# The first two groups' matrices fetched one by one with register addresses, beside the gathers, in a kernel on one core

## The chip, the core and the metric

The kernel runs on one core of a Trainium2 chip. The metric is the device time of one execution in microseconds (us). The core has five engines with an instruction queue each: TensorE (PE in the rows; its weight loads are PEld), VectorE (DVE), ScalarE (ACT), GpSimd (POOL) and SyncE (SP), which only waits and issues transfers. They meet at semaphores. Transfers (DMAs) are issued by SP, ACT or POOL and carried by 16 DMA engines that all of them share.

## The reference, cut to what is computed

```python
# x (32, 32, 256) f32; itok (32,) int32 in 1..198; L0_cond_weights (200, 32, 32)
w = weights[conditions]                       # one 32x32 matrix per batch, chosen by itok
y = einsum('bct,bcd->bdt', x, w)              # the mixing, 32 batches
h = silu(y @ w_gate) * (y @ w_up)             # w_gate, w_up (256, 1024)
h_sparse = of every 4 neighbours of h along the last axis, the 2 largest in magnitude, the others 0
out = x + h_sparse @ w_down                   # w_down (1024, 256)
```

## The kernel before

The 32 batches are eight groups `g` of four (`NG = 8`, `NB = 4`), since four batches of 32 channels fill 128 partitions. Groups 0 to 3 are half 0 and groups 4 to 7 half 1; each half is 512 columns wide (`TH`). The 256 entries of `T` are two blocks `k` of 128. Every product of the two big layers is made of float32r parts: a value is split into a high part, written by ScalarE as a copy (`high_weights`, `high_y`), and a low part, the difference, written by VectorE (`low_weights`, `low_y`), and three of the four products of the parts are summed.

The start of the program, on which everything here rests, runs as follows.

- SP issues `cond` (the chosen rows' numbers), `x[0]` (half 0 of x, 512 KB) and the k = 0 piece of `w_gate` (256 KB, lines 173 to 176). It then waits until the first gather has landed (`mix_in[0]`) and issues the k = 1 piece and the first 512 KB of `w_up`, waits for the latter, and issues `x[1]`, the second halves of the weights and `w_down`.
- VectorE adds the two halves of `cond` to row numbers (line 439). GpSimd then issues two indirect DMAs (line 206), one per half: each gathers for all 16 batches of its half the matrices, in chunks, from `table`. VectorE puts the gathered chunks in place with a 32x32-block transpose (line 351, signalled by `transposed`) and spreads them over a block diagonal (`mix_diag`, line 359, in three spans of groups).
- TensorE starts with 12 matmuls on a zeroed tile `warm` (line 520), whose results nobody reads. It then waits for the first `w_gate` piece's high part and mixes half 0: for k = 0 batch by batch, 16 matmuls of 32 rows and 32 columns (`mixing_by_batch`, line 529), for k = 1 with the block diagonal, one matmul per group (`mixing`, line 543). `mixed` counts when a k is ready; ScalarE and VectorE split it into `y_hl`.
- `first_gates` (line 570) makes the gate products of pairs 0 and 1 together (12 matmuls of 512 columns), and `gate_up(n)` (line 558) the others: 16 pairs `n`, each one block of 128 hidden columns in one half. Half 1 is mixed ahead of pair 3 (`MIX_PAIR`). For each pair ScalarE makes the silu, VectorE the product, and both then find the two largest of four. The down products (line 600) close the program.

In a row of the trace a float32 matmul of the mixing appears as two records, so 16 matmuls stand there as 32.

All orders are written out by hand; each engine works its instructions off in that order. The weight pieces and who waits for them come from this table and function:

```python
PIECES = [(0, w, k, k + 1) for w in range(2) for k in range(KT)] + \
         [(q, w, 0, KT) for q in range(1, NQ) for w in range(2)]
def pieces_until(q, w, k):
    return 1 + max(i for i, piece in enumerate(PIECES) if piece[:2] == (q, w) and piece[2] <= k)
```

Of the kernel before, what the change touches and what calls it, by code (L numbers as in the profile page):

```python
# [5 lines left out]
NQ = 2  # L6
M = 4
CHUNKS = 8

def adaln_ffn(nc: bass.Bass, x: bass.AP, x_t: bass.AP, cond: bass.AP, table: bass.AP,
              w_gate: bass.AP, w_up: bass.AP, w_down: bass.AP, out: bass.AP):

# [9 lines left out]
    P = 128  # L23
    i32 = mybir.dt.int32
    _, _, GH, T = x.shape
    NH = 2
# [10 lines left out]
    WARM_START = 12  # L37
    LAST = len(UNITS) - 1
    MIX_PAIR = 3
    SENT = 2  # L40
# [7 lines left out]
    with ctx:  # L48
# [27 lines left out]
        mix_w = h[:, 1, 1, 0:NG * D].rearrange("p (g o d) -> p g o d", o=1, d=D)  # L76
# [12 lines left out]

        cond_in = sem("cond_in")  # L90
        x_in = [sem(f"x_in{i}") for i in range(NH)]
        w_in = [[None, sem("gate_in1")], [sem(f"up_in{q}") for q in range(NQ)]]
# [6 lines left out]
        transposed = sem("transposed")  # L99
        diag_done = sem("diag_done")  # L100
# [38 lines left out]
        def split_y(part, half, k, end):  # L139
# [5 lines left out]
        SPANS = [slice(0, 2), slice(2, 4), slice(4, 8)]  # L145

        PIECES = [(0, w, k, k + 1) for w in range(2) for k in range(KT)] + \
                 [(q, w, 0, KT) for q in range(1, NQ) for w in range(2)]

        def pieces_until(q, w, k):  # L150
            return 1 + max(i for i, piece in enumerate(PIECES) if piece[:2] == (q, w) and piece[2] <= k)

        GATE_PIECES_END = PIECES.index((1, 0, 0, KT)) + 1

# [4 lines left out]
        UNFINISHED = 3  # L159
# [7 lines left out]
        def raw_piece(q, w, k, end):  # L167

            return raw_w[w][:, q, k:end].rearrange("p k (j g) -> p k j g", j=M)

        @block.sync
        def _(sp):
# [11 lines left out]
            sp.dma_start(raw_w[0][:, 1], w_gate[1].rearrange("k p n -> p k n")).then_inc(w_in[0][1], 16)  # L184
            sp.dma_start(raw_w[1][:, 1], w_up[1]).then_inc(w_in[1][1], 16)
# [4 lines left out]
            for i, (half, k, begin, end, _) in enumerate(OUTPUTS[:-1]):  # L190
                if i != UNFINISHED:
# [37 lines left out]
        def _(act):  # L229
# [43 lines left out]
            for k in range(KT):  # L273
                high_weights(*PIECES[k])
                high_y(*Y_PIECES[k])
# [398 lines left out]
```

## Time and profile before

| | us |
|---|---|
| three timed runs | 80.46, 80.88, 80.88 (median 80.88) |
| the profiled execution's own time | 80.44 |
| its span, first to last instruction | 78.6 |
| TensorE busy | 74.5 (95% of the span) |
| VectorE, ScalarE, GpSimd busy | 62.1, 41.7, 8.6 |

The profiled execution's time is 1.84 us longer than its span; that part lies outside of what the instructions show. Busy time of an engine says how full it is, and the chain of work that ended last says on which engine the end depends. A row of the timeline gives start, duration, engine, line, operation, the tile written and the tiles read, the count that was merged into the row, and in brackets how long the engine had been idle and what released it. SPq and ACTq are the sequencers' own rows: there a DMA row is the issuing, not the transfer.

### The profile page before, as it was taken

What the parts mean: (1) busy time and instruction counts of PE and PEld (TensorE: products, weight loads), DVE (VectorE), ACT (ScalarE), POOL (GpSimd) and SP (SyncE); (2) the same over time, 40 slices, a digit from 0 to 9 for tenths busy, and PEclk for the clock granted to TensorE, in tenths of its full rate; (3) what the DMA queues carried; (4) which work ended last, traced back from release to release, by engine and by line L of the source; (5) the groups of instructions that cost most, each with busy time, mean ns of one, the idle gap of its engine ahead of it and who ended that gap; (6) DMA issues with size and microseconds to landing.
All of it is one profiled execution on the core that took longest, in us unless ns stands there. A gap on an engine that the chain in (4) does not pass through costs nothing.

```text
span 78.6 us, 1020 instructions
## 1 busy us (share of the span) xinstructions
PE 74.5 (95%) x362; PEld 59.5 (76%) x362; DVE 62.1 (79%) x91; ACT 41.7 (53%) x61; POOL 8.6 (11%) x18
## 2 busy tenths in 40 slices
PE   3999999999999999999999999999999999999950
PEld 1338778888888888888888888888888888888840
DVE  0017691699879999599999979999999999994460
ACT  6122753869453375599897769789380402730000
POOL 5550000000000013000713000006200000000000
PEclk9999999999999999999999999999999999999999
DMA  0857559984900004900099990003995000003333
GB/s 1 250 183 201 232 154 381 413 377 92 425 33 0 0 0 79 188 0 0 15 194 200 194 198 13 4 0 60 200 177 96 0 0 0 8 0 138 137 142 118
DMA packets 3221, 9.64 MB, mean 123 GB/s; under 512 B 496, under 2 KB 752, under 8 KB 2960
## 3 DMA queue, kind: packets, MB, share of 16 engines
q0 software_dynamic: 928, 3.28, 21.9%
q1 hardware_dynamic: 2144, 6.16, 21.8%
q10 hardware_dynamic: 144, 0.13, 0.5%
q8 instruction: 3, 0.05, 0.2%
q14 instruction: 2, 0.02, 0.1%
HBM read 5.38 MB, written 1.05 MB: 82 GB/s over the span
## 4 chain that ended last, share of the span: by engine, by line
PE 95%; POOL 1%; DVE 1%; issue 0%; POOLq 0%
PE banks L558 52%; PE banks L600 28%; PE banks L520 6%; PE banks L543 4%; PE banks L570 4%; PE banks L529 1%; POOL warm L199 1%; DVE gate_raw L435 1%; POOLq L663 0%
## 5 line engine op out<-in xcount | busy, mean ns | idle before, releaser
L558 PE MATMUL banks<-y_hl,up_hl 128*128 128x512 f32 x96 | 24.2, 389 | 0.0
L600 PE MATMUL banks<-h_hl,down_hl 128*128 128x512 f32 (+1 forms) x102 | 22.0, 376 | 0.0
L558 PE MATMUL banks<-y_hl,gate_hl 128*128 128x512 f32 x84 | 21.4, 390 | 0.0
L600 PEld LDWEIGHTS banks<-h_hl,down_hl 128*128 128x128 f32 x102 | 18.5, 188 | 3.6
L558 PEld LDWEIGHTS banks<-y_hl,up_hl 128*128 128x128 f32 x96 | 18.0, 188 | 3.8
L558 PEld LDWEIGHTS banks<-y_hl,gate_hl 128*128 128x128 f32 x84 | 15.7, 188 | 3.2
L243 ACT ACTIVATE silu<-banks 128x512 f32<-128x512 f32 x16 | 9.6, 597 | 12.4 <-PE banks L558 12.1
L384 DVE TENSOR_TENSOR h<-banks,silu 128x512 f32<-128x512 f32 x12 | 8.3, 689 | 4.4 <-ACT silu L243 4.4
L264 ACT ACTIVATE h_hl<-h 128x1024 fp32r<-128x1024 f32 (+1 forms) x8 | 6.7, 843 | 3.9 <-DVE h L420 3.9
L420 DVE SCALAR_TENSOR_TENSOR h<-count,h 128x512 f32<-128x512 bf16 x12 | 7.9, 687 | 0.1
L520 PE MATMUL banks<-warm 128*128 128x512 bf16 x12 | 4.8, 586 | 1.3 <-POOL warm L199 1.3
L250 ACT ACTIVATE x_sb<-h 128x512 f32<-128x512 f32 x8 | 4.9, 626 | 1.7 <-DVE h L384 1.7
L435 DVE TENSOR_TENSOR gate_raw<-banks,gate_raw 128x512 f32<-128x512 f32 (+1 forms) x6 | 3.5, 602 | 2.4 <-PE banks L600 2.3
L214 POOL DMA_DIRECT2D down_hl<-down_raw x2 | 1.8, 919 | 31.5 <-ACT down_hl L259 31.5
L219 POOL DMA_DIRECT2D h_hl<-h x4 | 3.7, 928 | 13.4 <-ACT h_hl L268 13.4
L395 DVE TENSOR_TENSOR far<-x_sb 128x1024 bf16<-128x1024 f32 x4 | 4.9, 1222 | 0.2
L395 DVE TENSOR_TENSOR far<-a_even 128x1024 bf16<-128x1024 f32 x4 | 4.9, 1220 | 0.2
L520 PEld LDWEIGHTS banks<-warm 128*128 128x128 bf16 x12 | 1.6, 141 | 4.1 <-issue 2.7
L268 ACT ACTIVATE h_hl<-h 128x1024 fp32r<-128x1024 f32 x4 | 4.2, 1054 | 0.0
L233 ACT ACTIVATE gate_hl<-gate_raw 128x512 fp32r<-128x512 f32 (+1 forms) x3 | 2.3, 771 | 3.6 <-DMA gate_raw<-in_w_gate 3.6
L264 ACT ACTIVATE h_hl<-up_raw 128x1024 fp32r<-128x1024 f32 x2 | 2.1, 1054 | 3.2 <-DVE up_raw L420 3.2
L351 DVE STREAM_TRANSPOSE h<-h 128x128 f32<-128x128 f32 x2 | 0.8, 406 | 3.1 <-DMA h<-in_table,rows_sb 3.1
(39 smaller groups left out, 68.1 us busy)
## 6 DMA issues: line engine op xcount, KB each, us to landing
h_hl<-h POOLq DMA_DIRECT2D x4, 512.0 KB, 6.1
x_sb<-in_x SPq DMA_DIRECT2D x2, 512.0 KB, 3.4
up_raw<-in_w_up SPq DMA_DIRECT2D x2, 512.0 KB, 4.7
down_raw<-in_w_down SPq DMA_DIRECT2D x1, 1024.0 KB, 7.8
gate_raw<-in_x_t SPq DMA_DIRECT2D x1, 1024.0 KB, 4.8
down_hl<-down_raw POOLq DMA_DIRECT2D x2, 512.0 KB, 5.0
out<-gate_raw SPq DMA_DIRECT2D x3, 256.0 KB, 2.4
gate_raw<-in_w_gate SPq DMA_DIRECT2D x2, 256.0 KB, 3.3
```

Source lines behind the costliest of these rows:

```text
L219: pool.dma_start(h_hl[:, u, LO, j:end], hs[u][:, j:end], accum_op=ALU.add).then_inc(h_lo_sent[u][j // 2], 16)
L243: nc.scalar.activation(silu[:, n % 3], gate_bank(n), ACT.Silu).then_inc(silu_done, 1)
L250: nc.scalar.activation(a[u % 2][:, j], hs[u][:, j], ACT.Abs).then_inc(abs_done, 1)
L264: nc.scalar.activation(h_hl[:, u, HI, j:end], hs[u][:, j:end], ACT.Copy).then_inc(h_hi, 1)
L268: nc.scalar.activation(h_hl[:, u, LO, j:end], hs[u][:, j:end], ACT.Copy, scale=-1.0).then_inc(h_neg, 1)
L384: nc.vector.tensor_tensor(hs[u][:, j], up_bank(n), silu[:, n % 3], ALU.mult).then_inc(h_done, 1)
L395: step(nc.vector.tensor_tensor(far[:, j - 2::2], au[:, 0:2], au[:, j:j + 1].broadcast_to([P, 2, TH]), ALU.is_ge))
L420: nc.vector.scalar_tensor_tensor(hs[u][:, j], count[:, j], bound, hs[u][:, j], op, ALU.mult).then_inc(masked, 1)
L435: nc.vector.tensor_tensor(xt_sb[:, k, cols], bank[:, begin:end], xt_sb[:, k, cols], ALU.add).then_inc(out_done, 1)
L520: nc.tensor.matmul(gate_bank(0), warm[:, 0:P], warm[:], start=True, stop=True)
L558: last = nc.tensor.matmul(dst, w_hl[w][:, s, q, k, j], y_hl[:, m, half, k], start=i == 0, stop=i == len(terms) - 1)
L600: last = nc.tensor.matmul(bank[:, begin:end], down_hl[:, s, q, j, k * P:(k + 1) * P], h_hl[:, u, m, j, begin:end], start=(q, j, m, s) == f ...
```

## The change

Groups 0 and 1 of half 0 (eight batches; `EARLY = 2`) get their matrices in another way. The host also sends the list of chosen numbers (`cond_list`) and the unchunked table (`matrices`). ScalarE reads the four numbers of group 0 from `cond_list` in HBM into registers, and issues one 4 KB transfer per batch whose source address is a register. SP does the same for group 1, after its first three transfers. `early_in[g]` counts the four transfers of a group. The host rolls the list of the gathers by two groups, so that the first gather brings groups 2 to 5 and the second groups 6, 7, 0 and 1 (the last two into room that nobody reads).

Around that, five things move:

- VectorE zeroes `warm` in place of GpSimd, and TensorE's warm matmuls are 8 in place of 12.
- ScalarE's table load and first silu stand behind its four transfers.
- TensorE's mixing of half 0 goes group by group: group 0 for both k, then group 1, and then groups 2 and 3, for k = 0; only these two wait for the gathered matrices (`transposed`). The k = 1 matmuls of groups 1 to 3 follow. VectorE makes the diagonal of group 0 alone first, and those of groups 1 to 3 in one instruction behind the transpose.
- The first half of the weights comes in smaller pieces: for k = 0 and k = 1 of `w_gate` only the first 256 of 512 columns (128 KB each in place of 256 KB), then the first 256 columns of `w_up`, then the rest of both. There are seven pieces in place of six, and ScalarE and VectorE split them in that order. The second half comes in four transfers in place of two.
- The last output transfer but one is issued by ScalarE and the last by SP; before, ScalarE issued the last.

```diff
-    WARM_START = 12
+    WARM_START = 8
+    EARLY = 2
...
+        PIECES = [(0, 0, k, k + 1, 0, 2) for k in range(KT)] + [(0, 1, 0, KT, 0, 2)] + \
+                 [(0, w, 0, KT, 2, M) for w in range(2)] + [(1, w, 0, KT, 0, M) for w in range(2)]
+        LATER = KT + 3
...
-        SPANS = [slice(0, 2), slice(2, 4), slice(4, 8)]
+        SPANS = [slice(0, 1), slice(1, GH), slice(GH, NG)]
...
             sp.dma_start(x_sb[:, 0:GH, :], x[0]).then_inc(x_in[0], 16)
-            sp.dma_start(raw_w[0][:, 0, 0], w_gate[0, 0]).then_inc(first_in[0], 16)
+            sp.dma_start(raw_w[0][:, 0, 0, 0:2 * P], w_gate[0, 0, 0]).then_inc(first_in[0], 16)
+            _, chosen = nc.values_load_multi_w_load_instructions(
+                cond_list[:, NB:2 * NB], engines=(mybir.EngineType.SP,),
+                skip_runtime_bounds_check_because="the transfers check their own bounds")
+            for b in range(NB):
+                sp.dma_start(mix_w[b * C:(b + 1) * C, 1, 0],
+                             matrices[bass.ds(chosen[b], 1)].rearrange("o c d -> (o c) d")).then_inc(early_in[1], 16)
             sp.wait_ge(mix_in[0], 16)
             for k in range(1, KT):
-                sp.dma_start(raw_w[0][:, 0, k], w_gate[0, k]).then_inc(first_in[k], 16)
-            sp.dma_start(raw_w[1][:, 0], w_up[0]).then_inc(w_in[1][0], 16)
-            sp.wait_ge(w_in[1][0], 16)
+                sp.dma_start(raw_w[0][:, 0, k, 0:2 * P], w_gate[0, 0, k]).then_inc(first_in[k], 16)
+            sp.dma_start(raw_w[1][:, 0, :, 0:2 * P], w_up[0, 0].rearrange("k p n -> p k n")).then_inc(up_in, 16)
+            for w, weights in enumerate((w_gate, w_up)):
+                sp.dma_start(raw_w[w][:, 0, :, 2 * P:4 * P],
+                             weights[0, 1].rearrange("k p n -> p k n")).then_inc(rest_in[w], 16)
+            sp.wait_ge(up_in, 16)
             sp.dma_start(x_sb[:, GH:NG, :], x[1]).then_inc(x_in[1], 16)
...
-            nc.gpsimd.memset(warm[:], 0.0).then_inc(warm_zero, 1)
...
+            _, chosen = nc.values_load_multi_w_load_instructions(
+                cond_list[:, 0:NB], engines=(mybir.EngineType.Activation,),
+                skip_runtime_bounds_check_because="the transfers check their own bounds")
+            for b in range(NB):
+                act.dma_start(mix_w[b * C:(b + 1) * C, 0, 0],
+                              matrices[bass.ds(chosen[b], 1)].rearrange("o c d -> (o c) d")).then_inc(early_in[0], 16)
             act.wait_ge(warm_zero, 1)
             nc.scalar.activation(silu[:, 0, 0:2], warm[:, 0:2], ACT.Silu).then_inc(table_loaded, 1)
...
+            nc.vector.memset(warm[:], 0.0).then_inc(warm_zero, 1)
             dve.wait_ge(cond_in, 16)
+            dve.wait_ge(blocks_marked, 1 + NB)
             nc.vector.tensor_tensor(rows_sb[:], cond_sb[:, 0:NH], cond_sb[:, NH:2 * NH], ALU.add).then_inc(rows_done, 1)
-            dve.wait_ge(blocks_marked, 1 + NB)
+            diagonal(SPANS[0])
             transpose_rows(0)
-            diagonal(SPANS[0])
             diagonal(SPANS[1])
...
+            def first_mixing():
+                mixing_by_batch(0)
+                mixing(0, 1)
+                mixing_by_batch(1)
+                for g in range(EARLY, GH):
+                    last = mixing_by_batch(g)
                 last.then_inc(mixed, 1)
+                for g in range(1, GH):
+                    last = mixing(g, 1)
+                last.then_inc(mixed, 1)
```

How the first instructions of ScalarE stand before, in its queue from the start on. `silu<-warm` is the instruction that makes the table be loaded, `gate_hl<-gate_raw` the high part of the first weight piece:

```order
L272 ACT_TABLE_LOAD
L272 ACTIVATE silu<-warm 128x2 [waits warm_zero]
L233 ACTIVATE gate_hl<-gate_raw 128x512 [waits first_in0]
L237 ACTIVATE y_hl<-banks 128x512 [waits mixed]
L233 ACTIVATE gate_hl<-gate_raw 128x512 [waits first_in1]
```

And how they stand now; `h<-in_matrices` is one batch's matrix, and an ISA row the arithmetic on its address:

```order
L302 TENSOR_LOAD in_cond_list_ptr
L302 TENSOR_LOAD in_cond_list
L306 ISA
L306 DMA h<-in_matrices 32x32
L306 ISA
L306 DMA h<-in_matrices 32x32
L306 ISA
L306 DMA h<-in_matrices 32x32
L306 ISA
L306 DMA h<-in_matrices 32x32
L309 ACT_TABLE_LOAD
L309 ACTIVATE silu<-warm 128x2 [waits warm_zero]
```

Ten rows now stand ahead of the table load; the high part of the first weight piece, now 128x256, follows behind the silu as before.

How TensorE's queue stands before, from its start to the mixing of k = 1:

```order
L520 MATMUL banks<-warm 128x512 [waits warm_zero]
L520 MATMUL banks<-warm 128x512 x11
L529 MATMUL banks<-h,x_sb 128x32 [waits transposed,x_in0,w_hi]
L529 MATMUL banks<-h,x_sb 128x32 x15
L543 MATMUL banks<-h,x_sb 128x128 [waits diag_done,x_in0]
```

And the same place now:

```order
L560 MATMUL banks<-warm 128x512 x7
L572 MATMUL banks<-h,x_sb 128x32 [waits x_in0,early_in0,w_hi]
L572 MATMUL banks<-h,x_sb 128x32 x3
L582 MATMUL banks<-h,x_sb 128x128 [waits diag_done]
L572 MATMUL banks<-h,x_sb 128x32 [waits early_in1]
L572 MATMUL banks<-h,x_sb 128x32 x3
L572 MATMUL banks<-h,x_sb 128x32 [waits transposed]
L572 MATMUL banks<-h,x_sb 128x32 x3
L572 MATMUL banks<-h,x_sb 128x32 [waits transposed]
L572 MATMUL banks<-h,x_sb 128x32 x3
L582 MATMUL banks<-h,x_sb 128x128 [waits diag_done]
```

The wait for `transposed`, which stood ahead of all 16 small matmuls, now stands ahead of the last eight, and there are waits for the two groups' transfers ahead of the others.

## Rows read from the trace of the kernel before

**Rows 1.** The page: busy time by engine, and the last chain's shares.

```profile
PE 74.5 (95%) x362; PEld 59.5 (76%) x362; DVE 62.1 (79%) x91; ACT 41.7 (53%) x61; POOL 8.6 (11%) x18
...
PE 95%; POOL 1%; DVE 1%; issue 0%; POOLq 0%
```

**Rows 2.** The last chain in order of time (start, duration, what), its first pieces.

```profile
1.33 4.83 PE banks L520 x12
6.16 0.08 issue
6.24 1.09 PE banks L529 x32
7.33 1.09 PE banks L543 x8
8.42 2.91 PE banks L570 x12
11.33 5.46 PE banks L558 x24
```

**Rows 3.** The timeline up to 5.5 us, from several engines.

```profile
0.75 0.52 POOL L199 MEMSET warm<- 128x512 bf16 x1 [0.29 <-POOLq L663]
0.75 0.38 SPq L173 DMA_DIRECT2D cond_sb<-in_cond  x1
0.75 1.28 ACT L272 ACT_TABLE_LOAD   x1 [0.75 <-PEq L663]
1.19 0.42 SPq L175 DMA_DIRECT2D x_sb<-in_x  x1
...
1.66 0.42 SPq L176 DMA_DIRECT2D gate_raw<-in_w_gate  x1
...
2.05 0.20 ACT L272 ACTIVATE silu<-warm 128x2 f32<-128x2 bf16 x1
...
2.86 1.19 POOL L206 DMA_INDIRECT h<-in_table,rows_sb  x1 [0.97 <-DVE rows_sb L439]
...
5.14 0.15 PEld L520 LDWEIGHTS banks<-warm 128*128 128x128 bf16 x1 [0.28 <-issue]
5.37 0.63 ACT L233 ACTIVATE gate_hl<-gate_raw 128x512 fp32r<-128x512 f32 x1 [3.12 <-DMA gate_raw<-in_w_gate]
5.57 0.10 PEld L520 LDWEIGHTS banks<-warm 128*128 128x128 bf16 x1 [0.27 <-issue]
```

**Rows 4.** The timeline from 5.6 to 8.5 us, from several engines.

```profile
5.60 0.33 SPq L180 DMA_DIRECT2D gate_raw<-in_w_gate  x1
5.68 0.41 DVE L351 STREAM_TRANSPOSE h<-h 128x128 f32<-128x128 f32 x1 [3.11 <-DMA h<-in_table,rows_sb]
...
6.21 1.01 PEld L529 LDWEIGHTS banks<-h,x_sb 32*128 32x128 f32 x32 [0.54 <-ACT gate_hl L233]
...
7.39 0.60 ACT L237 ACTIVATE y_hl<-banks 128x512 fp32r<-128x512 f32 x1 [1.39 <-PE banks L529]
8.09 0.69 DVE L373 TENSOR_TENSOR y_hl<-banks,y_hl 128x512 fp32r<-128x512 f32 x1 [0.60 <-ACT y_hl L237]
...
8.44 0.63 ACT L233 ACTIVATE gate_hl<-gate_raw 128x512 fp32r<-128x512 f32 x1 [0.45 <-DMA gate_raw<-in_w_gate]
```

**Rows 5.** DMA issues: KB each and median us from issue to landing.

```profile
x_sb<-in_x SPq DMA_DIRECT2D x2, 512.0 KB, 3.4
...
out<-gate_raw SPq DMA_DIRECT2D x1, 128.0 KB, 1.9
...
cond_sb<-in_cond SPq DMA_DIRECT2D x1, 2.0 KB, 1.6
```

**Rows 6.** Stretches, us: each engine's busy time (records), granted clock, DMA share, GB/s.

```profile
3.00:4.00 1.00, 1.00 (x4) 0.44 (x3) 0.00 (x0) 0.00 (x0) 1.00 (x1) 1.00 1.02 375
4.00:4.50 0.50, 0.50 (x3) 0.17 (x2) 0.00 (x0) 0.00 (x0) 0.20 (x2) 1.00 1.00 389
...
5.00:5.50 0.50, 0.50 (x2) 0.15 (x1) 0.00 (x0) 0.13 (x1) 0.35 (x1) 1.00 0.03 8
```

**Rows 7.** Shapes in the first 20 us: busy us, mean ns of one.

```profile
L366 DVE TENSOR_TENSOR gate_hl<-gate_raw,gate_hl 128x512 fp32r<-128x512 f32 x2 | 1.4, 688 | 0.4 <-ACT gate_hl L233 0.4
...
L233 ACT ACTIVATE gate_hl<-gate_raw 128x1024 fp32r<-128x1024 f32 x1 | 1.1, 1052 | 0.0
...
L359 DVE TENSOR_TENSOR h<-h,own_block 128x256 f32<-128x256 f32 x2 | 0.8, 422 | 0.0
```

**Rows 8.** The timeline where the up weights are split, and VectorE's first product.

```profile
9.67 1.15 ACT L233 ACTIVATE up_hl<-up_raw 128x512 fp32r<-128x512 f32 x2
...
13.44 0.69 DVE L384 TENSOR_TENSOR h<-banks,silu 128x512 f32<-128x512 f32 x1 [1.75 <-ACT silu L243]
```

**Rows 9.** The end of VectorE's work, and the outputs.

```profile
68.65 1.90 DVE L426 TENSOR_TENSOR h_hl<-h,h_hl 128x512 fp32r<-128x512 f32 x3
...
75.91 0.42 DVE L435 TENSOR_TENSOR gate_raw<-banks,gate_raw 128x256 f32<-128x256 f32 x1 [0.21 <-PE banks L600]
76.37 0.37 ACTq L335 DMA_DIRECT2D out<-gate_raw  x1
```

More of the change, by code:

```diff
@@ L99, in adaln_ffn @@
         transposed = sem("transposed")
+        early_in = [sem(f"early_in{g}") for g in range(EARLY)]
         diag_done = sem("diag_done")
@@ L142, in adaln_ffn @@
         Y_PIECES = [(0, k, k + 1) for k in range(KT)] + [(1, 0, KT)]
-        SPANS = [slice(0, 2), slice(2, 4), slice(4, 8)]
[L147 to L153, printed above, removed]
+        SPANS = [slice(0, 1), slice(1, GH), slice(GH, NG)]
+        GATE_PIECES_END = PIECES.index((1, 0, 0, KT, 0, M)) + 1
         OUTPUTS = [(0, 0, 0, TH, y_banks[:, 0]), (0, 1, 0, TH, y_banks[:, 1]),
@@ L189, in _ @@
             sp.dma_start(xt_sb, x_t).then_inc(xt_in, 16)
-            for i, (half, k, begin, end, _) in enumerate(OUTPUTS[:-1]):
-                if i != UNFINISHED:
+            for i, (half, k, begin, end, _) in enumerate(OUTPUTS):
+                if i not in (UNFINISHED, LEFT):
                     cols = slice(half * TH + begin, half * TH + end)
@@ L273, in _ @@
             for k in range(KT):
-                high_weights(*PIECES[k])
+                high_weights(k)
                 high_y(*Y_PIECES[k])
-            for piece in PIECES[KT:2 * KT]:
-                high_weights(*piece)
+            for i in range(KT, LATER):
+                high_weights(i)
             act.wait_ge(table_loaded, 1)
@@ L446, in _ @@
                 low_y(k)
-            for i in range(KT, 2 * KT):
+            for i in range(KT, LATER):
                 low_weights(i)
@@ L533, in mixing, with mixing_by_batch @@
-            def mixing(half, first=0):
-                pe.wait_ge(x_in[half], 16)
-                if half > 0:
-                    pe.wait_ge(y_lo, KT * half)
-                for k in range(first, KT):
-                    for i in range(GH):
-                        g = half * GH + i
-                        span = [groups.start <= g < groups.stop for groups in SPANS].index(True)
-                        if k == first and g == SPANS[span].start:
-                            pe.wait_ge(diag_done, span + 1)
-                        last = nc.tensor.matmul(y_banks[:, k, i * P:(i + 1) * P],
-                                                x_sb[:, g, k * P:(k + 1) * P],
-                                                mix_diag[:, g].rearrange("p b d -> p (b d)"),
-                                                start=True, stop=True)
+            def mixing_by_batch(g):
+                if g < EARLY:
+                    pe.wait_ge(early_in[g], 16 * NB)
+                else:
+                    pe.wait_ge(transposed, 1)
+                if g == 0:
+                    pe.wait_ge(x_in[0], 16)
+                for b in range(NB):
+                    rows = slice(b * C, (b + 1) * C)
+                    last = nc.tensor.matmul(banks[:, b, g * D:(g + 1) * D], x_sb[rows, g, 0:P],
+                                            mix_w[rows, g, 0], start=True, stop=True)
+                return last
@@ L547, in mixing, with second_mixing @@
+            def second_mixing():
+                pe.wait_ge(x_in[1], 16)
+                pe.wait_ge(y_lo, KT)
+                for k in range(KT):
+                    for g in range(GH, NG):
+                        last = mixing(g, k)
                     last.then_inc(mixed, 1)
@@ L613, in _ @@
                 if n == MIX_PAIR:
-                    mixing(1)
+                    second_mixing()
                 gate_up(n)
@@ L656 @@
         "cond": cond,
-        "table": table,
-        "w_gate": columns(inputs["L0_ffn_w_gate"]).transpose(0, 2, 1, 3),
+        "cond_list": _np.asarray(inputs["itok_B_1_198"]).reshape(1, B),
+        "table": chunks,
+        "matrices": table,
+        "w_gate": columns(inputs["L0_ffn_w_gate"]),
         "w_up": columns(inputs["L0_ffn_w_up"]),
```

105 lines of the change are left out of this document (62 added, 43 removed).

## The prediction, as it was put on record

> **What bounds the kernel now.** I read first the page's busy times and the shares of the last chain [rows 1]: TensorE is busy 95% of the span, and 95% of the chain lies on it. Then the chain in order of time [rows 2]: it enters TensorE at 1.33 us and from there goes from one group of matmuls to the next without a wait; to the end it leaves TensorE only for the last addition. So time is gained or lost only where TensorE's real work starts, or where it would come to wait. The change touches the start, so the timeline up to 8.5 us comes next [rows 3, 4]. Four things are to be seen there. The 12 warm matmuls are loaded 0.43 us apart (5.14 and 5.57) and end at 6.16. The gather starts on GpSimd at 2.86 and VectorE's transpose of what it brought runs 5.68 to 6.09. ScalarE's high part of the first weight piece runs 5.37 to 6.00, when that piece has landed. TensorE's first real weight load stands at 6.21. Three causes thus meet within 0.16 us, the warm matmuls (6.16), the gathered matrices (6.09) and the weight piece (6.00), and an edit that moves one alone brings nothing. Behind that, mixing takes 1.09 + 1.09 us and the first gates start at 8.42 [rows 2]. Those need the split y: ScalarE has it at 7.99 [rows 4], so TensorE's own 2.18 us of mixing is what ends last.
>
> **The edits with one answer.** The weight piece of 128 KB in place of 256 KB: the DMA engines were full and moved 375 to 389 GB/s [rows 6], so 0.128 MB less ahead of it is 0.34 us, and it lands at 5.37 - 0.34 = 5.03. Its high part has 256 columns: 1.05 us for 1024 against 0.63 for 512 [rows 7, 3] makes 0.42 for 256. The memset of the warm tile goes from GpSimd (0.52 us, [rows 3]) to VectorE, for which I take 0.25; TensorE starts at about 1.05 instead of 1.33. Eight warm matmuls at 0.43 end at 4.5. GpSimd's gather waits for the row numbers, not for its memsets, and stays at 2.86. The smaller later pieces cost VectorE and ScalarE one more instruction for the same number of elements, some 0.1 to 0.2 us. It is hidden by VectorE's wait of 1.75 us ahead of its first product, and the gate halves that were whole before now come behind the first half of up, which is why ScalarE's work on up, 9.67 before, can start earlier [rows 8]. Without that cover it would cost its 0.2. SP's two more issues at up to 0.47 stand ahead of w_down, which is needed long after. The swap of the last two outputs changes who issues, ScalarE in 0.37 before [rows 9]; SP's issues take 0.33 to 0.42 [rows 3, 4]: nothing.
>
> Then four transfers. SP's issues stand 0.44 and 0.47 us apart [rows 3]; with the address arithmetic I take 0.45. Behind them wait, on the same engine, the table load (1.28) and the silu (0.20) [rows 3], which before ran in the shadow of the transfers, and then the first high part, for which TensorE waits. The sum: 0.75 + 1.2 + 4 x 0.45 + 1.28 + 0.20 + 0.42 = 5.65. With the 0.12 us from the transpose's end to the first load (6.09 to 6.21, [rows 4]) TensorE begins at 5.77. The cover is nearly gone: the piece has landed at 5.03 and ScalarE comes free at 5.23. Group 0's transfers, the last of them issued at 3.30, land within 1.6 us if nothing is in the way, at 4.9, and by 6.1 if they are slowed to the gather's 2.6 or a little more; its diagonal of 128 columns takes under 0.42 [rows 7]. I take it as hidden.
>
> **SP's path, and the sum.** SP's third issue ends at 2.08 [rows 3]. Loads until 3.28, the fourth matrix issued at 3.28 + 3 x 0.45 = 4.63, landed 1.6 later [rows 5] at 6.23; the DMA engines are nearly idle by then (share 0.03 at 5.0 to 5.5, [rows 6]). TensorE goes on with group 1 at 6.35. By ScalarE's path it would be there at 5.77 + 0.27 (a quarter of the 1.09 of k = 0) + 0.27 (a quarter of the 1.09 of k = 1) = 6.31, so SP's path is last by 0.04. Groups 1 to 3 take three quarters of 1.09, to 7.17; the gathered matrices (6.09) are no longer waited for. The three k = 1 matmuls take 0.82 more, to 7.99. The split y is there at 7.17 + 0.06 + 0.60 [rows 4], about 7.9 with its signal, in time. The first gates start at 7.99 instead of 8.42: 0.43 us earlier. Behind SP's loads waits the k = 1 piece of w_gate; SP is free at 5.1, ahead of the 5.60 at which it was issued before, and half the size it lands earlier than the 8.44 of before [rows 4, 5]. From there on TensorE is full, and VectorE, whose first product comes 1.75 us of waiting after its last split [rows 8], moves with it, as does its end, which at 70.55 (68.65 + 1.90) lies over 5 us ahead of the last addition [rows 9].
>
> Against the profiled execution's own time: 80.44 - 0.43 = 80.0. That execution is the fastest of those shown; two of three runs are at 80.88, and 0.42 us is one warm matmul. If those runs had one slot more of slow matmuls ahead of the mixing, the change takes that away too, for its warm matmuls end 1.3 us before they are needed; I don't add it.
>
> **The ends.** If the loads are as short as the lower bound, the gather decides again: transpose ended at 6.09, half of the small matmuls (0.55) and three big ones (0.82) make 7.58, a gain of 0.84, and up to 0.34 more if the gather lands earlier by the smaller weight piece. The sum breaks even where both loads together take 1.63 us, and loses 1.57 at 3.2.
>
> **The rivals.**
> (a) *Nothing moves.* The loads take 1.25 to 2.0 us, so the matrices that were to come early come with the gathered ones or just behind, and the small pieces of work moved ahead only fill the wait. 80.1 to 80.8. For it: its whole cause is an operation that no row shows, and my sum is only 0.4 away. Against: even at 1.2 there are 0.43 in hand.
> (b) *The loads are long.* Beyond 2.0 us, ScalarE and SP hold up the first mixing, each behind its own loads; at 2.6 the first gates start at 9.39, and the time is 81.4. The page cited above would make it this. For it: two trips to memory in series; against: 2.6 is more than 1.6 of the whole small transfer without its issue, twice.
> (c) *TensorE's clock.* The granted clock stands at 1.00 in all stretches [rows 6], but warm matmuls of 512 columns come every 0.43 us, which is 1.2 GHz, and gates (12 in 2.91, [rows 2]) every 0.24, close to 2.4. So TensorE began at the low level and had risen by its first real work, after 4.9 us without a pause. Now it stops at 4.5 and idles for 1.3 us. If it is not at the high level then, half the speed costs the mixing (1.64 us of TensorE's work from 6.35) another 1.64 and, at worst, the gates 5.12 - 2.91 = 2.2 more; I take the first, 81.6. This is the rival on the other side: one mechanism, at 4.5 to 5.8 us, and it decides as soon as the rise is missed before 6.3 (break-even: 0.86 us of work at the low level). For it: the pause is new and half-speed work is in the trace; against: 3.4 us of work still stand ahead of the pause. The skill's "TensorE: Matmul & The Clock Gate", section "What's actually happening", says that "the default state is throttled, and activity releases the throttle"; by that the pause counts against the rise, and rows here can't say how much.
>
> **How the numbers follow.** About 0.5% (0.4 us) is what a measurement of this kernel can tell from no change. Forecast, a gain of 0.4 to 1.2: 0.50. Rival (a), within 0.4: 0.25. Rival (b): 0.11. Rival (c): 0.14. The predicted time is the forecast's, 80.0. The low end takes in the short loads and a part of the earlier gather, 79.3. The high end must take in (b) and most of (c), 81.7. Faster 0.50, same 0.25, slower 0.25. The forecast's own range is 79.3 to 80.1.
>
> **What would show it.** ScalarE's table load should start near 3.75 us (0.75 + 3.0), each 0.1 us later being 0.1 us of load time; its first high part should end near 5.65; TensorE's first small matmuls should stand at 5.8 with a pause behind the warm ones, those of group 1 at 6.35, and the first gates at 8.0, at 0.24 us each. A table load at 5 or later means (b); gates at over 0.4 us each mean (c); a first gate at 8.4 means (a). The prediction is wrong in its core if TensorE waits later, for the split of the smaller pieces, where I see no wait.

## The result, and the profile after

The changed kernel takes 83.60 us (median of 6 runs, 83.12 to 84.93) against 80.75 us before (6 runs, 80.46 to 80.88): 1.0346 of the time before, 95% interval 1.0301 to 1.0390. It is slower by 2.85 us where 0.43 us less was forecast, and outside the range. The profiled execution took 83.12, with a span of 81.3 (before 78.6). Wherever TensorE's clock can be lost, single executions of one kernel lie up to 3.7 us apart; there the single times stand beside the median.

The last chain of the changed kernel in order of time (start, duration, what), answering to [rows 2]:

```profile
2.14 1.80 SPq L198
...
4.06 0.49 SPq L198
...
6.30 1.50 DMA h<-in_matrices
...
7.84 0.87 PE banks L572 x24
8.71 1.55 PE banks L582 x6
10.26 3.69 PE banks L625 x12
13.95 5.45 PE banks L613 x24
```

The chain no longer lies on TensorE from 1.33 on. It runs through SP: its first register load takes 1.80 us, its second 0.49, then come the four small transfers, and the last of these lands at 7.80. The first gates (L625) start at 10.26 in place of 8.42, and take 3.69 in place of 2.91. That is 1.84 and 0.78, together 2.62 of the 2.7 us by which the span grew. From 13.95 on every piece is as long as before.

The timeline of the changed kernel, answering to [rows 3, 4]:

```profile
2.34 1.83 ACTq L306 DMA_DIRECT2D h<-in_matrices  x4
...
4.20 1.28 ACT L309 ACT_TABLE_LOAD   x1 [4.20 <-issue]
...
4.74 1.87 SPq L202 DMA_DIRECT2D h<-in_matrices  x4
...
5.61 0.40 ACT L264 ACTIVATE gate_hl<-gate_raw 128x256 fp32r<-128x256 f32 x1
6.02 0.29 DVE L399 TENSOR_TENSOR h<-h,own_block 128x128 f32<-128x128 f32 x1 [3.44 <-DMA h<-in_matrices]
...
6.09 0.42 PE L572 MATMUL banks<-h,x_sb 32*128 32x32 f32 x8 [1.28 <-ACT gate_hl L264]
6.23 0.40 DVE L388 STREAM_TRANSPOSE h<-h 128x128 f32<-128x128 f32 x1
...
7.84 0.87 PE L572 MATMUL banks<-h,x_sb 32*128 32x32 f32 x24 [0.91 <-DMA h<-in_matrices]
```

TensorE pauses twice: 1.28 us behind the warm matmuls, for ScalarE's first high part, and 0.91 us for group 1. The gathered matrices, transposed by 6.63 (6.23 + 0.40), wait for group 1, which stands ahead of them in TensorE's queue. VectorE took up that transpose right behind group 0's diagonal, so this trace shows only that the gather had landed by 6.23, not when.

Stretches of the changed kernel, answering to [rows 6] (busy time of TensorE, its loads, VectorE, ScalarE, GpSimd with records; granted clock; DMA share; GB/s):

```profile
2.00:3.00 1.00, 1.00 (x4) 0.40 (x3) 0.16 (x1) 0.00 (x0) 0.12 (x1) 1.00 0.72 201
3.00:4.00 1.00, 1.00 (x4) 0.34 (x3) 0.00 (x0) 0.00 (x0) 1.00 (x1) 1.00 0.95 337
...
8.00:9.00 1.00, 1.00 (x26) 0.96 (x27) 0.78 (x2) 0.22 (x1) 0.00 (x0) 0.85 0.80 264
9.00:10.00 1.00, 1.00 (x7) 1.00 (x6) 0.59 (x1) 0.68 (x2) 0.00 (x0) 0.50 1.10 288
10.00:12.00 2.00, 2.00 (x7) 1.61 (x6) 1.50 (x4) 1.71 (x4) 0.00 (x0) 0.50 0.83 253
```

While SP's first load ran, from 2.14 to 3.94, the DMA engines were at a share of 0.72 to 0.95. Behind the pauses the granted clock falls to 0.50, which is 1.2 GHz, and comes back past 12 us. The six k = 1 records took 1.55 us in it and the gates 3.69; in the run keep_clock below, at the full clock, they took 0.86 and 2.87. So the clock cost 0.69 + 0.82 = 1.5 us of this execution, and the late matrices most of the rest.

### The profile page after: what moved, and what is told of

It reads as the page before. It is cut to its first block, busy times and chain, and to the rows that moved or that the text cites. A ratio compares the mean times of both kernels' runs of the same rounds, so it can differ in the third digit from the quotient of the medians.

```text
span 81.3 us, 1052 instructions
## 1 busy us (share of the span) xinstructions
PE 75.1 (92%) x358; PEld 60.6 (74%) x358; DVE 62.4 (77%) x93; ACT 41.5 (51%) x62; POOL 8.1 (10%) x17
## 3 DMA queue, kind: packets, MB, share of 16 engines
q1 hardware_dynamic: 3680, 6.18, 22.3%
q0 software_dynamic: 928, 3.28, 21.2%
HBM read 5.41 MB, written 1.05 MB: 79 GB/s over the span
## 4 chain that ended last, share of the span: by engine, by line
PE 87%; SPq 6%; DMA 2%; issue 1%; DVE 1%
PE banks L613 50%; PE banks L655 27%; PE banks L625 5%; PE banks L582 4%; SPq L198 3%; DMA h<-in_matrices 2%; SPq L202 2%; PE banks L572 1%; DVE gate_raw L474 1%; SPq L197 1%; SPq L196 1%; SPq L194 0%
## 5 line engine op out<-in xcount | busy, mean ns | idle before, releaser
L613 PE MATMUL banks<-y_hl,gate_hl 128*128 128x512 f32 x84 | 21.4, 390 | 0.0
L399 DVE TENSOR_TENSOR h<-h,own_block 128x128 f32<-128x128 f32 (+2 forms) x3 | 1.5, 514 | 4.7 <-DMA h<-in_matrices 4.7
L560 PE MATMUL banks<-warm 128*128 128x512 bf16 x8 | 3.6, 628 | 1.2 <-DVE warm L477 1.2
L582 PE MATMUL banks<-h,x_sb 128*128 128x128 f32 x24 | 4.1, 324 | 0.0
L625 PE MATMUL banks<-y_hl,gate_hl 128*128 128x512 f32 x12 | 4.0, 498 | 0.0
L268 ACT ACTIVATE y_hl<-banks 128x512 fp32r<-128x512 f32 (+1 forms) x3 | 2.2, 736 | 3.4 <-PE banks L572 2.8
```

Of the source, the lines that this page charges most:

```text
L582: return nc.tensor.matmul(y_banks[:, k, i * P:(i + 1) * P], x_sb[:, g, k * P:(k + 1) * P], mix_diag[:, g].rearrange("p b d -> p (b d)"), s ...
L613: last = nc.tensor.matmul(dst, w_hl[w][:, s, q, k, j], y_hl[:, m, half, k], start=i == 0, stop=i == len(terms) - 1)
L625: nc.tensor.matmul(gate_bank(n), w_hl[0][:, s, 0, k, n], y_hl[:, m, 0, k], start=i == 0, stop=i == len(terms) - 1)
```

## The experiments

Three theories stood against each other. L: the register loads hold up SP and ScalarE. C: the pauses cost TensorE its clock. Q: the eight small transfers themselves are in the way of others. Where a run's name begins with `fixed`, the small transfers read fixed rows of the table, so groups 0 and 1 are mixed with other matrices than the chosen ones; the loads and the arithmetic on addresses are left out with that.

### keep_clock: the pauses filled

```diff
-    WARM_START = 8
+    WARM_START = 12
...
                 mixing(0, 1)
+                warm_up(4)
                 mixing_by_batch(1)
```

> The changed kernel with 12 warm matmuls in place of 8 and four more between group 0's mixing and group 1's, so that TensorE has work in the two pauses; nothing else is changed. If the pauses cost the clock (theory C), the granted clock stays 1.00, the six k = 1 records take 0.82 us instead of 1.55 and the first 12 gates 2.91 instead of 3.69: gates start near 9.5 and the time falls by about 1.5 us to 82.1, and what is left over before (1.3 us) is the loads. If the clock falls for another reason (theory O), the time stays at 83.6. If all is the loads (theory L), it stays too, since the matrices still come at 7.8.

Measured: 81.61 us, ratio 1.0146 (1.0104 to 1.0189). The last chain:

```profile
6.87 0.86 PE banks L560 x4
7.73 0.83 PE banks L572 x24
8.56 0.86 PE banks L582 x6
9.43 2.87 PE banks L626 x12
```

The filling matmuls end where group 1 arrives (7.69), so they delay nothing by more than 0.04. The clock stays, the gates start at 9.43 as expected, and the time falls by 1.6 us (by the two ratios, 1.0346 and 1.0146) to 2.0 us (by the two medians, 83.60 and 81.61). So theory C holds for 1.6 to 2.0 of the 2.85 us. 0.8 to 1.5 us over before are left (the interval of the ratio), and these are not the clock: its gates start 1.01 us later than in [rows 2], at the full clock.

### before_warm8 and after_warm12: which pause costs the clock

The kernel before with `WARM_START = 8`, and the changed kernel with `WARM_START = 12`.

> The kernel before with 8 warm matmuls in place of 12 and nothing else: they end near 4.75, so TensorE pauses for 1.4 us ahead of the mixing, which starts at 6.2 as before. Theory C1 (the one pause after the warm matmuls is enough to lose the clock): the granted clock falls to 0.50 for some 3 us behind the mixing, the gates take 3.7 or more, and the time is 81.8 to 83. Theory C2 (it takes the second pause too, the wait for group 1): the clock stays 1.00 and the time is 80.5 or a little less.

Measured: 82.88 us, the four executions 80.51, 81.93, 83.83 and 84.05, beside 80.55 for before. The last chain of its profile:

```profile
6.31 1.93 PE banks L529 x32
8.25 2.00 PE banks L543 x8
10.25 4.40 PE banks L570 x12
```

Against [rows 2] the three pieces are longer by 0.84, 0.91 and 1.49, in all 3.2 us: TensorE ran at half speed from its first real matmul, behind a pause of 1.39 us. The expectation had the clock fall behind the mixing; here it had not risen before the gates. Its stretches from 6 to 14 us show a granted clock of 1.00 all the same:

```profile
7.00:8.00 1.00, 1.00 (x24) 1.00 (x23) 0.56 (x1) 0.00 (x0) 0.00 (x0) 1.00 0.95 318
```

Theory C1 holds in three of the four executions: one edit of one number, 12 to 8, costs up to 3.5 us in an execution and nothing in another.

> The changed kernel with 12 warm matmuls in place of 8 and nothing else (no filling ones in the second pause, the wait for group 1 from 6.9 to 7.8). If the pause behind the warm matmuls alone costs the clock (theory C1), this is as fast as keep_clock, 81.6. If the second pause costs it too (theory C2), it lies between, 82.2 to 83.6.

Measured: 82.43 us, the four executions 81.50, 81.79, 83.06, 83.14. Two are as fast as keep_clock, and two are 1.3 to 1.6 us slower. In the profiled one, one of these two, TensorE has no pause ahead of the mixing (its warm matmuls run until it starts, at 6.10) and one of 0.77 us ahead of group 1; behind that the clock stands at 0.50 from 10 to 12 us and the gates take 4.15:

```profile
8.58 1.07 PE banks L582 x6
9.65 4.15 PE banks L625 x12
```

So either pause can cost the clock, and neither does so each time. A cause for which execution is hit was not tested.

### before_loads: what the loads and transfers cost in the queues

Both loads and the eight transfers added to the kernel before, into a tile that nobody reads, in front of SP's wait for the gather and of ScalarE's first silu.

> The kernel before with both register loads and the eight small transfers added at the places they have in the change, into room that nobody reads. It prices what stands in the queues: ScalarE's table load starts 3.45 us later and its first high part ends at about 6.35 instead of 6.00; SP issues the k = 1 piece at about 6.7 instead of 5.6, so its high part comes at 10.1 and the split of y behind it at 10.7. Theory L: 0.3 us at the start and 0.6 at the k = 1 gates, 81.4 in all. If the queues' load has cover, 80.8.

Measured: 81.85 us, ratio 1.0189 (1.0113 to 1.0266), 0.45 more than expected of theory L. Its last chain:

```profile
2.15 2.00 SPq L180
...
4.26 0.49 SPq L180
...
6.87 2.77 DMA gate_raw<-in_w_gate
...
9.65 0.63 ACT gate_hl L243
...
10.91 1.63 PE banks L586 x6
```

SP's first load takes 2.00 us here, and its second 0.49 with the DMA engines at a share of 0.97 (4.0 to 4.5 us) and 1.03 (4.5 to 5.0). So a share near 1 does not by itself make a load long. The k = 1 piece behind it is issued 1.27 us later than in [rows 4], and TensorE waits for what is made of it in the middle of the gates. In the change this second damage does not show; that its piece is half as large and its gates are later anyway is the likely reason, not tested alone. The start is later too: the gather, which VectorE waited for at 5.68 in [rows 4], lands 0.56 us later beside the small transfers, in a kernel whose own matrices still come by it.

```profile
6.24 0.40 DVE L367 STREAM_TRANSPOSE h<-h 128x128 f32<-128x128 f32 x1 [3.67 <-DMA h<-in_table,rows_sb]
```

### sp_loads_early: the loads moved ahead of the bulk

keep_clock with SP's loads between `cond` and `x[0]`.

> The run keep_clock with SP's two register loads moved between its first transfer (cond) and its second (x); the small transfers stay behind the third. On SP the first load took 1.80 us behind three transfers, on ScalarE 0.86 with none ahead. Theory T (a load takes longer while the core's transfers are under way): 0.9 + 0.5 here, the last small transfer is issued near 5.0 and landed by 6.6; x and the weight piece come 1.4 us later, at about 6.0 and 6.5, first high part 6.9; gates near 8.6 to 9.0, 80.8 to 81.2. Theory S (SP's loads are slow in themselves): 1.8 + 0.5 again, and the time does not fall below 81.6.

Measured: 82.80 us, ratio 1.0264 (1.0215 to 1.0312). The size of the loads came out as theory T has it, their cause did not get decided: SP's `cond` issue ends at 1.15 and the next transfer starts at 2.66, so both loads with their gaps took 1.5 us, against 2.4 in the changed kernel. But two things changed at once, the traffic and the two large transfers that SP had issued ahead of the load, and the second load takes 0.48 to 0.50 wherever it is seen. Which of the two makes the first one long stays open. The time did not fall. Its chain says why:

```profile
3.83 3.21 DMA h<-in_matrices
...
7.13 0.42 PE banks L572 x8
```

Group 0's last transfer, issued by ScalarE at 3.8 as in the changed kernel, now lands 3.2 us after that in place of some 2.2 (at 7.04, not 6.02), while x and the weight piece, issued 1.4 to 1.5 us later, are still moving. SP's transfers for group 1 are issued 1.05 us earlier, from 3.69 on, and their matrices are there at 7.86, no earlier than in the changed kernel (7.89):

```profile
7.86 0.56 DVE L399 TENSOR_TENSOR h<-h,own_block 128x384 f32<-128x384 f32 x1 [0.19 <-DMA h<-in_matrices]
```

The clock was lost as well in this profile. What a small transfer takes depends on what else is under way.

### fixed_rows, fixed_keep, fixed_warm12: no loads at all

The loads deleted and the rows fixed; then with the warm matmuls of keep_clock; then with 12 and no filling ones.

```diff
-            _, chosen = nc.values_load_multi_w_load_instructions(...)
...
-                              matrices[bass.ds(chosen[b], 1)].rearrange("o c d -> (o c) d")).then_inc(early_in[0], 16)
+                              matrices[b:b + 1].rearrange("o c d -> (o c) d")).then_inc(early_in[0], 16)
```

> The changed kernel without the register loads: the eight transfers have fixed rows as their source, so groups 0 and 1 are mixed with other matrices than the chosen ones; all instructions but the loads and the address arithmetic stay. Theory L (the loads hold up SP by 2.5 us and ScalarE by 1.6): SP's last small transfer is issued at 3.5, landed by 5.1 to 5.6, the ScalarE path ends at 5.5, TensorE mixes from 5.6 on and the gates start near 7.8: 79.8. Theory C alone (the pause after the warm matmuls, now 1.1 us, is enough to lose the clock): the loads gone bring back 2.0 us, but the gates still run at half the clock, 81.4 or more. Theory P (the smaller pieces are what costs): no nearer than 82.5.

> The run with fixed source rows (no register loads; groups 0 and 1 are mixed with other matrices than the chosen ones), with 12 warm matmuls and four more between group 0 and group 1. There the gather landed at 6.9 in place of 5.6, and the clock fell. If the late gather is an effect of the eight small transfers in the DMA queues (theory Q), it is late again: transpose ends near 7.3, the gates start at 8.9 with the clock at 1.00, span 79.2, time 81.0, slower than before by 0.6% although no load is left. If it was an accident of that execution (theory A), the gates start at 7.9 to 8.2 and the time is 79.9 to 80.2.

> The changed kernel with fixed source rows for the eight small transfers (no register loads; groups 0 and 1 are mixed with other matrices than the chosen ones) and 12 warm matmuls, without the filling ones of fixed_keep, whose TensorE never waited and so could not show what it would have waited for. Theory Q (the eight transfers hold up the gather): the gather lands at 6.7 to 6.9 again, gates start near 8.9 to 9.1, 80.9 to 81.2. Theory A (fixed_keep's time was only its filling matmuls): gather at 5.6, gates at 7.9 to 8.2, 79.9 to 80.3.

Measured: fixed_rows 83.70 (1.0404, 1.0360 to 1.0448), fixed_keep 81.71 (1.0111, 1.0057 to 1.0166), fixed_warm12 80.94 (1.0062, 1.0037 to 1.0087). The first is no faster than the changed kernel: without its loads, the clock is still lost (the gates take 4.45 us), in all four executions by their times (82.94 to 84.03). Four warm matmuls more, in fixed_warm12, take 2.8 us off it.

```profile
8.92 4.45 PE banks L619 x12
```

The second never let TensorE wait, so its filling matmuls hid the answer; the third gives it. Its timeline:

```profile
0.76 1.82 ACTq L300 DMA_DIRECT2D h<-in_matrices  x4
...
2.13 1.82 SPq L199 DMA_DIRECT2D h<-in_matrices  x4
...
6.07 0.29 DVE L393 TENSOR_TENSOR h<-h,own_block 128x128 f32<-128x128 f32 x1 [3.40 <-DMA h<-in_matrices]
...
6.88 0.35 SPq L204 DMA_DIRECT2D gate_raw<-in_w_gate  x1
6.89 0.41 DVE L382 STREAM_TRANSPOSE h<-h 128x128 f32<-128x128 f32 x1 [0.53 <-DMA h<-in_table,rows_sb]
```

ScalarE is done with issuing group 0's transfers at 2.58 (0.76 + 1.82), and the matrices are there at 6.07, when the changed kernel has them too (6.02), though it issues them 1.6 us later. And the gather, which landed at 5.68 in [rows 4], lands at 6.88. Theory Q holds: issued while x and the weight piece move, the small transfers land no earlier, and the gather lands 1.2 us later. Theory L alone would have given 79.8. That is the cost in this run; in the changed kernel, whose SP transfers start at 4.74, the gather had landed by 6.23 and was not what TensorE waited for.

What the loads cost by themselves can be read from one pair: after_warm12 and fixed_warm12 differ only in the loads, the arithmetic on addresses and the rows read. The two executions of after_warm12 that kept their clock took 81.50 and 81.79, against 80.94 here; by the ratios (1.0135 and 1.0062) 0.6 us.

### fixed_one and fixed_start: fewer transfers, and earlier ones

Each group's four matrices by one transfer of 16 KB, at the places of the change, then both as ScalarE's first two instructions; 12 warm matmuls.

> As fixed_warm12, but each group's four matrices come by one transfer of 16 KB over all 128 partitions, at the same places in ScalarE's and SP's queues (other matrices than the chosen ones). If the number of small transfers is what holds up the gather: it lands at 5.6 to 5.9, gates at 8.0 to 8.3, 80.0 to 80.4. If any transfer on these queues does it, the time is as in fixed_warm12.

> As fixed_one, but both groups' transfers are issued by ScalarE as its first two instructions, at 0.76 and 1.2, ahead of the bulk of x and the weights. This is the most that early matrices can bring. They land by 3.5; TensorE can start when the weight piece's high part is there, 5.6 to 5.7, and has half the mixing behind it when the gather's transpose ends at 5.95. Theory G (early matrices shorten the start): gates at 7.5 to 7.7, 79.5 to 79.9. Theory N (the start is set by gather, weight piece and warm matmuls alike, whatever comes early): 80.2 or more, as in pieces_only.

Measured: fixed_one 80.68 (1.0026, 0.9998 to 1.0054), fixed_start 80.59 (1.0006, 0.9976 to 1.0037). In fixed_one the gather is back in time (5.63), and the gates start at 8.64 in place of 8.88. So the eight small transfers are what pushed it, by their number or by the time over which they are issued: two are out by 2.56, eight by 3.95, and group 0's one is out before x's is issued. The runs don't part these.

```profile
2.13 0.43 SPq L198 DMA_DIRECT2D h<-in_matrices  x1
...
5.62 0.33 SPq L202 DMA_DIRECT2D gate_raw<-in_w_gate  x1
5.63 0.41 DVE L378 STREAM_TRANSPOSE h<-h 128x128 f32<-128x128 f32 x1 [2.71 <-DMA h<-in_table,rows_sb]
```

That is what the Trainium skill's "DMA: Bandwidth & Descriptors", section "Rules for kernel authors", says of many small transfers, to join them into one large; this trace agrees (6.88 and 5.63). With one register address for each matrix they stay four transfers for a group. fixed_start has group 0's matrices at 2.6 us and gains nothing (before took 80.40 beside it): its last chain is TensorE alone, its 12 warm matmuls ending at 6.18.

```profile
1.20 4.98 PE banks L550 x12
6.18 0.35 PE banks L562 x8
6.53 0.42 PE banks L572 x2
6.95 0.80 PE banks L562 x24
7.75 0.86 PE banks L572 x6
8.62 2.91 PE banks L615 x12
```

### fixed_start_w10: is there anything in early matrices?

> As fixed_start (both groups by one 16 KB transfer each at the very start, fixed rows, so other matrices than the chosen ones) with 10 warm matmuls in place of 12: they end near 5.5, so TensorE no longer works them off until 6.2 while everything it needs is there. Theory G (early matrices shorten the start once the warm matmuls don't hide it): TensorE starts at 5.75, gates at 8.0 to 8.2, 0.4 us less than fixed_start, 80.0 to 80.2. Theory N (no gain is left in early matrices): 80.5 or more, by a clock that comes late.

Measured: 81.27, the four executions 80.45, 80.58, 81.96 and 83.88. The two undisturbed ones are as fast as before (ratio 0.9995, 0.9946 to 1.0043), the others did not keep the clock (the profiled one, 81.96, has the granted clock at 0.50 from 8 to 10 us; that of the other is judged by its time alone). TensorE starts at 5.94, bound by the weight piece's high part (ScalarE 5.47 to 5.89), 0.30 earlier than before, and the order by groups costs what that brings. 8 small records take 0.42 and 24 take 0.80, where [rows 2] has 1.09 for 32; two large ones take 0.42 and six 0.86 (fixed_start), where it has 1.09 for 8: 2.50 in place of 2.18. Theory G's 80.0 to 80.2 was not reached in any execution. Even matrices that are there at 2.6 us, without a load, are worth nothing measurable in this kernel as it orders its mixing. Early matrices mixed in the order of before, all of k = 0 first, were not run.

### group0_only: ScalarE's half alone

`EARLY = 1`, the list rolled by one group, no loads and no small transfers on SP, 12 warm matmuls.

> Only group 0 comes early, by ScalarE (the list of the gathers is rolled by one group); SP has no loads and no small transfers; 12 warm matmuls. ScalarE's table load still stands behind its two loads and four transfers. Theory L (the loss is SP's path, ScalarE's is nearly free): group 0 from 6.0, the others from about 6.6, gates near 8.2, SP's k = 1 piece at 5.6 as in pieces_only: 80.2 to 80.5. Theory Q (four small transfers are enough to hold up the gather): transpose past 6.8, gates past 8.5, 80.9 or more.

Measured: 80.98, ratio 1.0046 (1.0017 to 1.0075), which is theory Q's time (80.9 or more), but not by its mechanism: the transpose ends at 6.65, not past 6.8, and TensorE does not wait for it. TensorE has no pause, its warm matmuls end at 6.45 in the profile; group 0's matrices are there at 6.04, and the gather lands at 5.87 in place of 5.53 as in pieces_only. Four small transfers delay it by 0.3 here (before_loads had 0.56), eight by 1.3. What costs is the order by groups: its four pieces of mixing take 2.43 us, those of pieces_again, whose warm matmuls end at the same time (6.48), take 2.11, and the profiled executions took 80.96 and 80.53. With ScalarE's half alone the change is slower too.

### pieces_only, pieces_again, pieces_w11: the rest of the change

The smaller weight pieces, the memset on VectorE and the swap of the outputs, with all matrices gathered and mixed in the order of before, and 12 warm matmuls (11 in the last).

```diff
-    EARLY = 2
+    EARLY = 0
...
-                mixing_by_batch(0)
-                mixing(0, 1)
-                mixing_by_batch(1)
-                for g in range(EARLY, GH):
+                for g in range(GH):
                     last = mixing_by_batch(g)
```

> The smaller weight pieces, their order, the memset on VectorE and the output swap of the change, without the early matrices: all groups come by the gathers, the mixing is in the order of before, 12 warm matmuls. If the pieces are harmless, as I put it: 80.4 to 80.9, ratio 0.995 to 1.00, since warm matmuls and gather still set the start. If they are part of the loss (theory P): over 81.2.

> The kernel of pieces_only once more, on the chip and in the call of the three above, for a firmer ratio: all theories expect 0.995 to 1.000 of before, 80.1 to 80.5.

> pieces_only with 11 warm matmuls. In its second profile the 12 end at 6.48, 0.5 us behind the transposed matrices, in the first at 5.63. If the warm matmuls' end is what spreads the times, 11 take up to 0.43 us off the slower executions: median 80.0 to 80.1. If a pause of that size loses the clock: some executions over 81.

Measured: 80.25 (0.9975, 0.9950 to 1.0000) and a second time 80.20 (0.9960, 0.9939 to 0.9981), with 11 warm matmuls 80.11, 80.22, 80.48 and 83.77. This part of the change is a small gain, 0.2 to 0.3 us, clear of noise in the second measurement only, and it is the fastest of the kernels run that mix with the chosen matrices. The weight piece's high part ends at 5.60 now (5.18 + 0.42), but TensorE starts at 6.04 behind the transpose in the profile where the warm matmuls end at 5.63, and behind the warm matmuls in the other, where they end at 6.48:

```profile
1.20 5.28 PE banks L548 x12
6.48 1.02 PE banks L560 x32
7.50 1.09 PE banks L570 x8
```

Eleven warm matmuls don't bring the median down (80.35), and one execution in four took 3.3 us more. It was not profiled; its time fits a clock that had not risen, as in before_warm8, and this is not shown.

## Why the prediction was wrong, point by point

**What bounds the kernel.** Right: three causes met within 0.16 us, and moving one brings nothing. The change moves all three, and the sum had TensorE start 0.47 us earlier (5.77 for 6.24). It began at 6.09. How little is to be had there fixed_start and fixed_start_w10 show: with the matrices at 2.6 us the warm matmuls (6.18) or the weight piece's high part (5.89) still hold TensorE.

**ScalarE's path.** Nearly right. The loads took 0.86 and 0.50 in keep_clock, where 0.6 each was put; the first rows of its chain are

```profile
0.76 0.86 ACTq L302
...
1.64 0.50 ACTq L302
```

Four transfers took 1.83 against 1.80, the table load stood at 4.20 against 3.75, the high part ended at 6.01 against 5.65, TensorE began at 6.09 against 5.77.

**SP's path.** This step failed first. The same two loads were put at 1.2 and took 2.4 on SP, because the first of them, 0.86 on ScalarE, took 1.80 behind three transfers; early on SP both took 1.5. The Trainium skill's page that the prediction weighed, "Runtime: NRT & Kernel Launch", section "The ~15µs preamble/postamble breakdown", has 1.3 for one: too long for each load on ScalarE and too short for SP's first, but the 2.6 for both at which it put the sum was near SP's 2.4. The last matrix landed at 7.80, not 6.23. Of these 1.57 us the loads are 1.27 (they ended at 4.55, not 3.28) and the issuing 0.40 (the fourth matrix 1.75 us behind them, not 1.35: 0.19 pass ahead of the first, and then they stand 0.52 apart, not 0.45); the landing, 1.50 for 1.6, gave 0.10 back. Why SP's first load was long stays open. I had priced it from `cond_sb`, issued into an idle memory, while the DMA engines are full from 3 to 4.5 us [rows 6]; that is a possible reason, not a shown one, for in before_loads the second load took 0.49 beside a share of 1.03.

**The landing and the cover.** Of the two ends for group 0's landing, 4.9 "if nothing is in the way" and 6.1, the second came: its transfers landed at about 6.0 whether their issuing ended at 2.6 or at 4.2. That it was hidden was a near thing: the matrices were there at 6.02, the high part at 6.01. The transposed gather was put at 6.09, as before; in the changed kernel it was there at 6.63, hidden by the wait for group 1, and with all eight small transfers in flight with the bulk (fixed_warm12) at 7.30. I had no price at all for the transfers on the others, though the DMA engines stood at a share of 1.02 [rows 6].

**The order by groups.** A quarter of 1.09 each, 0.54 for group 0, was put; 0.84 was measured (6.03 to 6.87 in keep_clock). Its first half lay in the shadow of the wait for group 1 in the change, but in all it is 0.3 us, and takes the gain away in fixed_start_w10.

**The clock.** This step failed too, and it is the larger part. The sum cut the warm matmuls from 12 to 8 and let TensorE pause, and put nothing for it; the price stood in rival (c), at 0.14. 1.5 us were lost in the profiled execution and 1.6 to 2.0 in the medians. (c) had the mechanism right, a pause costs the clock. Its 1.64 us was the mixing at half speed from 6.35, and that did not happen here: the 32 small records ran at full speed, the clock fell near 8.8, behind the second pause, and the six k = 1 records and the gates paid. So the size agrees by luck. Its sign (gates at over 0.4 us each) did not show either, 3.69 / 12 = 0.31, since the clock came back among the gates, and neither did that of (b), a table load at 5 or later (4.20).

(b) and (c) stood as cases that exclude each other. A long load makes a second pause, in which the clock can go as well (after_warm12), and the range ended at 81.7, the price of one alone. 80.0 + 1.4 + 1.6 = 83.0 is near the 83.12 of the profiled execution, in part by the luck above. But (c) needed no long load: fixed_rows has none and lost 2.8 us, and with 8 warm matmuls in the kernel before three of four executions were hit. A chance of 0.14 was too low.

**The rest.** The smaller pieces were put at nothing and brought 0.2 to 0.4%. The low end's 7.58 leaves one term unsaid: 6.09 + 0.55 + 0.82 is 7.46, and the other 0.12 is the step from the transpose to the first load. VectorE and the end moved with TensorE, as forecast: from the up products on, the chain up to the down products takes 42.68 us (42.71 before) and these 21.84 in both.

## What to carry to other kernels

Here small transfers that were issued 1.0 to 1.6 us earlier, beside the bulk, did not land earlier, and several of them pushed back the gather that mattered; ask what is moving in that stretch before you price an issue or a register load. Matmuls that only keep TensorE busy may be cut when real work takes their place, not when a wait does. In these runs a wait around the first real work brought the price of the clock on top of its own length in many executions, though not in all, so such rivals are to be added, not weighed against each other. Where three causes end together, test the ceiling first: one run with the new data there from the start would have shown that this idea had nothing to win.

## What the runs showed of the hardware that was not expected

- A register load from HBM took 0.86 us for the address and 0.50 for four words on ScalarE, and 1.77 to 2.00 and 0.49 on SP behind three transfers (after_warm12, the changed kernel, before_loads). The DMA engines were at a share of 0.72 to 0.95 during the first (the changed kernel) and up to 1.03 during the second (before_loads), which was no longer for it.
- A transfer of 4 KB with its address in a register is issued every 0.48 us on ScalarE's queue and every 0.50 to 0.54 on SP's; the last of four landed 1.5 us later with the DMA engines at a share of 0.3 (the changed kernel from 6 to 8 us), and 3.2 us later beside the bulk (sp_loads_early).
- The granted clock can read 1.00 from the start of a trace while TensorE runs at 1.2 GHz, as in the first warm matmuls of every profile (0.43 us for 512 columns) and in the profile of before_warm8 until its gates, 12 of which took 4.40 us. In these profiles it read 0.50 only where the clock had risen and fell. The spacing of equal matmuls is the surer sign.
- The time at which the clock rises differs between executions of one kernel: the 12 warm matmuls took 4.43 us in one profile of the same program and 5.28 in the other.
